# A spectral and mixture-of-experts kernel: width DFT and four centrings as four 64x64 tiles, first weight loads from the sixth sum on

## The reference

```python
x = x + _L0_conv_ref(_ln_c(x), L0_conv_w1_real, ...)   # 2D DFT, low modes times complex weights, inverse DFT
t = _to_tokens(x)
t = t + _L0_ffn_ref(_ln_t(t), L0_ffn_gate_w, ...)      # softmax over tokens, top 8 for each expert
x = _from_tokens(t, x)
x = x + _L1_conv_ref(_ln_c(x), L1_conv_w_d, ...)       # four sweeps, each row from the row before it
t = _to_tokens(x)
t = t + _L1_ffn_ref(_ln_t(t), L1_ffn_gate_w, ...)
```

## Time and profile before

| | |
|---|---|
| median of 3 runs | 577.56 us (576.42 to 582.18) |
| profiled execution, its own time | 579.15 us |
| its span, first to last instruction | 577.3 us |
| PE busy; PEld; DVE; ACT | 516.2; 462.0; 323.8; 275.8 us |
| first norm and width DFT in the trace | first centring 5.90 us, gate product 41.81 us |
| mean granted TensorE clock | 0.95 of full speed |

### The profile page before, as it was taken

How to read it: one execution, slowest core, us unless ns; L and a number is a source line. 1 busy time by engine, 2 the same in 40 slices (tenths; PEclk the granted TensorE clock), 3 DMA queues, 4 the chain that set the end, 5 groups by cost and what they waited for, 6 DMA issues and landing times.

```text
span 577.3 us, 25417 instructions
## 1 busy us (share of the span) xinstructions
PE 516.2 (89%) x11282; PEld 462.0 (80%) x11282; DVE 323.8 (56%) x767; ACT 275.8 (48%) x782; POOL 113.3 (20%) x240
## 2 busy tenths in 40 slices
PE   8878999768857999969999999889999999756997
PEld 8878998668747975859999888778899999756973
DVE  2757565833459537754544554445555445669626
ACT  3546554435577102654444444434446777748100
POOL 4000000000161000003333333643331033451000
PEclk9999999989996979988999999979999999976979
DMA  9940990051000000000000033410000244500007
GB/s 351 373 147 2 328 373 36 1 219 76 5 3 1 2 20 2 3 0 3 4 5 3 4 79 76 115 35 4 4 4 3 45 81 82 99 1 1 2 2 291
DMA packets 50259, 41.69 MB, mean 72 GB/s; under 512 B 44998, under 2 KB 45126, under 8 KB 48934
## 3 DMA queue, kind: packets, MB, share of 16 engines
q1 hardware_dynamic: 49304, 38.51, 20.8%
q0 software_dynamic: 704, 1.18, 0.9%
q10 hardware_dynamic: 144, 0.39, 0.2%
HBM read 27.49 MB, written 4.19 MB: 55 GB/s over the span
## 4 chain that ended last, share of the span: by engine, by line
PE 79%; DVE 8%; ACT 6%; POOL 4%; issue 3%; DMA 0%; SPq 0%; POOLq 0%; ACTq 0%; DVEq 0%
PE PS L766 40%; PE PS L550 6%; PE PS L494 5%; PE PS L735 5%; PE PS L591 3%; PE PS L532 3%; PE PS L685 3%; PE PS L473 2%; POOL RE L394 2%; PE PS L436 2%; POOL RCD L397 2%; PE PS L503 2%; DVE sums L1052 1%; PE PS L454 1%; PE PS L468 1%
## 5 line engine op out<-in xcount | busy, mean ns | idle before, releaser
L766 PE MATMUL PS<-RE,conv_sb 128*64 128x64 f32 x6048 | 231.2, 230 | 4.4 <-DVE RE L1151 4.0
L766 PEld LDWEIGHTS PS<-RE,conv_sb 128*64 128x64 f32 x6048 | 210.3, 139 | 25.4 <-DVE RE L1151 4.7
L901 ACT COPY PS<-convb_sb 128x64 f32<-128x64 f32 x504 | 108.2, 215 | 113.0 <-DVE RE L1163 102.6
L1163 DVE SCALAR_TENSOR_TENSOR RE<-PS,RCD 128x64 f32<-128x64 f32 x252 | 56.5, 224 | 58.3 <-PE PS L766 50.0
L406 POOL COPY RCD<-RE 128x128 f32<-128x128 f32 x126 | 37.1, 294 | 156.7 <-DVE RE L1163 156.6
L1163 DVE SCALAR_TENSOR_TENSOR RE<-PS,RE 128x64 f32<-128x64 f32 x126 | 32.6, 259 | 28.4 <-PE PS L766 21.0
L1163 DVE SCALAR_TENSOR_TENSOR RE<-PS,RB 128x64 f32<-128x64 f32 x126 | 28.3, 224 | 28.2 <-PE PS L766 28.2
L494 PE MATMUL PS<-warm 128*128 128x128 bf16 x418 | 35.6, 261 | 3.9 <-DVE warm L929 1.4
L494 PEld LDWEIGHTS PS<-warm 128*128 128x128 bf16 x418 | 32.6, 120 | 5.1 <-ACT RB L879 1.6
L394 POOL TENSOR_TENSOR RE<-RA 128x1024 f32<-128x1024 f32 x3 | 5.7, 1892 | 149.5 <-ACT RA L872 149.5
L550 PE MATMUL PS<-RE,RB 128*64 128x64 f32 x1024 | 32.2, 223 | 1.6 <-DVE RA L991 1.4
(11 more groups left out here) (117 smaller groups left out, 691.9 us busy)
## 6 DMA issues: line engine op xcount, KB each, us to landing
RE<-wspec SPq DMA_DIRECT2D x8, 2048.0 KB, 8.7
RA<-x_in SPq DMA_DIRECT2D x8, 512.0 KB, 7.4
RCD<-x_in SPq DMA_DIRECT2D x1, 4096.0 KB, 12.3
out<-RA SPq DMA_DIRECT2D x8, 512.0 KB, 2.7
RCD<-RB SPq DMA_DIRECT2D x58, 64.0 KB, 2.6
RE<-RCD SPq DMA_DIRECT2D x32, 80.0 KB, 2.6
conv_sb<-conv_w SPq DMA_DIRECT2D x1, 768.0 KB, 20.1
w_sb<-w SPq DMA_DIRECT2D x2, 264.0 KB
```

The lines of the kernel that those rows point to most:

```text
L766: m = pe.matmul(conv_bank(s, u, c)[o:o + OC], conv_sb[:, s, d, o:o + OC], prev, start=False, stop=(d == 2), skip_group_check=True)
L901: act.copy(banks_of, convb_sb[:, s:s + 1].unsqueeze(2).to_broadcast([P, c1 - c0, n])).then_inc(s_seed, 1)
L1163: dve.scalar_tensor_tensor(out=state[:, state_slot(s, u), b0:b1, 1:1 + HO], in0=conv_bank(s, u, c), scalar=0.0, in1=row_at(SRC[s], s, q, u ...
```

## The change

Three things change, all ahead of the gate product. The follower uses `quad` for all eight groups. The centring uses `quad` for groups 4 to 7 (`LN0_QUADS = 4`). Because `quad` splits the two halves over two banks, the normalisation of groups 4 to 7 and the drain read PSUM in another order; the drain becomes two copies of 512 columns. And chunks 0, 1 and 2 of the weights wait for sums 6, 7 and 8.

```diff
         def f1_pairs(g, i):
             o = RC.rearrange("p (t k r h) -> p t k r h", ...)[:, g // 4, :, :, 16 * (g % 4):16 * (g % 4) + 16]
-            return [(o, i.rearrange("p (h r k) -> p k r h", r=2, k=KY))]
+            return [(o[:, :, r].rearrange("p k (n a) -> p k n a", a=2),
+                     i.rearrange("p (a n r k) -> p r k n a", a=2, n=8, r=2)[:, r]) for r in range(2)]
...
-            for c in range(2):
-                sp.dma_start(RE[:, WCOLS * c:WCOLS * (c + 1)], wspec[c]).then_inc(s_wc[c], 16)
...
-            for c in range(2, NCH):
-                if c == 2:
-                    sp.wait_ge(s_sum, 8)
+            for c in range(NCH):
+                if c < 3:
+                    sp.wait_ge(s_sum, (6, 7, 8)[c])
...
-                        m = pe.matmul(blk(ln_slot(g), n), blk(RA, 8 * g + n), centre, start=True, stop=True)
+                        if g < LN0_QUADS:
+                            m = pe.matmul(blk(ln_slot(g), n), blk(RA, 8 * g + n), centre, start=True, stop=True)
+                        else:
+                            m = quad(2 * (g % 4), n, blk(RA, 8 * g + n), centre)
...
             def dft_w(g):
                 for n in range(8):
-                    m = pe.matmul(blk(ln_slot(g), n), blk(RD, 8 * g + n), fwd_w, start=True, stop=True)
+                    m = quad(2 * (g % 4), n, blk(RD, 8 * g + n), fwd_w)
...
+                            m = dve.tensor_tensor(
+                                tokens.rearrange("p (n a b c) -> p a n b c", a=2, b=2, c=C),
+                                ln_slot(g).rearrange("p (a n b c) -> p a n b c", a=2, b=2, c=C),
+                                r.rearrange("p (a n b) -> p a n b", a=2, b=2).unsqueeze(4).to_broadcast([P, 2, 8, 2, C]),
+                                ALU.mult)
```

## The result

The changed kernel takes 586.16 us, the median of 14 runs (582.05 to 590.8), against 576.39 us of the kernel before in the same 14 rounds: the ratio is 1.0159, with a 95% interval of 1.0123 to 1.0195. The ratios are taken over fast executions alone (without 590.8 us here), so they are not quite those of the medians. The changed kernel is slower, by 7 to 11 us. The forecast was 578.8 us and the range ended at 583, so both were wrong. The profiled execution took 587.83 us, and its span is 585.9 us against 577.3.

A forecast was written before the change was run, and what follows sets the result against it. PE and the normalisation ring bound the first stage by turns; after the change, late instruction blocks would. Quads -5.3 us and blocks +6.5 made 1.2 us more, against the median 577.56: 578.8 us, range 573 to 583.

The forecast's parts named there:

- The blocks: First stage: PE's 256-instruction blocks come late in followers 2 to 5 and 7, costing 6.5 us.
- What the loads do to a block: First stage: weight loads stretch a block from 3.9 us in quiet to about 5.5 us.
- The clock: First stage: PE idle waiting for a block drops to 1.2 GHz; 580.5 to 583.9 us, chance 0.15.
- the third rival: Clock falls in the wait for the last follower's block; 580.5 to 583.9 us, chance 0.15.
- the short fall: Half clock for 3.4 us over the last follower's end, gate product and row turns, losing 1.7 us.
- The half block: Four and a half added blocks move later block changes; inverse width DFT gaps change by 0.8 us either way.
- What the quads cost and save: First stage: 1.09 us from quad to quad against 1.79, at most 5.3 us gained.
- the gain with no late block: First stage: last follower ends at 35.4 instead of 40.71 us; 572.3 us, chance 0.15.
- The drain and the normalisation in halves: First stage: drain copies 1.16 us against 1.01, normalisation 1.23 against 1.22; extra 0.15 us paid once.
- The loads of weights: Moved chunks 0 to 2 land before their mixes need them, so waiting for them costs nothing.
- the price under load: While weights load, as in the mixing, a block takes about 5.5 us.

The follow-up runs named there:

- e3: The change, with weight chunks 0, 1 and 2 asked for only when all eight groups are drained; ratio 1.0034 to the kernel before.
- e9: The change, but with the last four centrings left whole, so followers alone are quads; ratio 0.9977 to the kernel before.
- e4: The kernel before plus 64 small dead matmuls (128 instructions) ahead of follower 6; ratio 1.0055.
- e11: The change plus 64 small dead matmuls between the last follower and the gate product, five whole blocks added; ratio 1.0153 to the kernel before.
- e6: The kernel before with followers and centrings 4 to 7 as two 64x128 tiles, plus 64 small dead matmuls ahead of the gate product; ratio 1.0289.
- e1: The change, with weight loads where they were before (chunks 0 and 1 right behind the image); ratio 1.0083 to the kernel before.
- e5: The kernel before with followers and centrings 4 to 7 as two 64x128 tiles, weight chunks early as before; ratio 1.0338.
- e12: The change, with followers alone as quads and the first chunks asked for only after the last drain; ratio 1.0034 to the kernel before.
- e2: The kernel before with only the weight loads moved to the sixth, seventh and eighth sums, tiles whole; ratio 0.9998.

## Why the prediction was wrong

- **The blocks.** Right in kind and in place: one for each lap, waits inside followers 2, 3, 4, 5 and 7, none in 6, 256 instructions apart. In quiet a block takes 3.55 to 3.83 us (e3), against 3.9 assumed; the first two came 1.2 and 1.3 us before their forecast times, with waits of 0.53 and 0.95 us where 1 us or more was forecast.
- **What the loads do to a block: mis-sized.** This is the first step that failed. Follower 4's block was priced at 4.15 us, since "the load is hardly under way", and those of 5 and 7 at 5.5 us, from the mixing. They took 6.02, 6.57 and 5.92: 18.5 us instead of 15.15. e3 shows that the loads are the cause. The first load was asked for at 25.15 us and the block at 25.21, and that block already took 6.02 us. The last block came at 43.72 us instead of 41.65.
- **The clock: the third rival came, earlier and longer, at its lower price.** The fall was priced for a wait of 3.3 us before the last follower, and given 0.15. It came three followers earlier, in the 3.51 us before follower 4's rest, which that mis-sized block had made so long; and it lasted 20.5 us, not 3.4 or 10. Its rows: quads of 1.9 us instead of 1.1, and row turns of 3.68 us, at 2.23 in e9. But up to the last block PE was held by its blocks and not by the slow quads, so that what the clock cost is some 1.7 us, the rival's price for the short fall. The chain to the first mix lost 5.2 us instead of 1.2: 2.1 us of the difference are the later last block, 1.7 the clock's. By that alone, 577.56 + 5.2 = 582.8 us, the time would have stayed in the range; what came behind the first mix took it out.
- **The half block: named, and not followed.** This is the second step that failed. The prediction saw that later block changes fall elsewhere and priced that at 0.8 us either way, by the inverse DFT alone. There it was 1.3 us more waiting than in the earlier trace rows. In the mixing, where weights are loading all the time, it cost some 3 us: 3.3 alone in e4 (ratio 1.0055), and 2.9 between the change and e11, where it is gone as in e6. This is the term that the sum lacked, and the largest behind the gate product. The same shows far behind, where it cost the change nothing (11.9 us late ahead of it and behind it): between 504 and 523 us the five kernels with a half block (the change, e1, e3, e4, e5) have issue waits of 1.19 to 2.4 us in the second layer's expert projections, and the other nine have none.
- **What the quads cost and save.** Right: 1.16 and 1.11 us each at the full clock. A last follower that ends at 35.4 us, the gain with no late block, was never seen. The nearest is e12, with followers alone as quads and no late block: its last one started at 35.53 us, at half the clock, and took 1.89.
- **The drain and the normalisation in halves.** Right, as the timelines of ACT and DVE show: two copies in 1.07 us (1.16 assumed), the normalisation in 1.22 us as in the earlier trace rows.

```profile
25.70 1.07 ACT L793 COPY RCD<-PS 128x512 f32<-128x512 f32 x2 [1.63 <-PE PS L454]
...
29.25 1.22 DVE L953 TENSOR_TENSOR RCD<-PS,rstd 128x1024 f32<-128x1024 f32 x1
```

- **The loads of weights.** Right that no mix waits for its chunk, and e2's whole time is that of before. Wrong that this settled the question: PE's blocks come later while weights move (e3), and with the new places of the loads the mixing waits some 1 us more (e2).

The rule of the Trainium skill's page "Runtime: NRT & Kernel Launch", section "Instruction fetch mechanics", that the fetch is mostly hidden, holds for the kernel before as a whole: it has three issue waits of over 0.15 us, in some 88 blocks (an estimate, 22564 / 256). It does not hold in the first stage of the change, where each of the five blocks from follower 2 on was waited for, 0.53 to 3.51 us.

What stays open: what decides whether the clock falls behind a wait, and why block changes half a block further on wait in the mixing, and those of before hardly do. In the change the late ones stand 6.1 to 6.4 us apart, the price under load, and those of before fall under the same loads. Which matmuls lie behind a change, and when the next chunk is asked for, both move with it; no run separates them.

## What to carry to other kernels

A tile that needs less of PE's time but four times the instructions is paid for by instruction blocks: count the instructions in each lap, compare 256 of them with the time that a block takes in that stage (here 3.6 to 3.8 us in quiet, 5.9 to 6.6 while large loads run), and expect a wait for the difference. Price what a wait can do to the clock along with the wait. And when an edit adds instructions ahead of a stage that runs close to this limit, add or take away whole blocks, or look at that stage again: half a block of dead work alone cost this kernel 0.55%.

## What the runs showed of the hardware

- The same 128 instructions of harmless work, hidden where they stand, made a stage that begins 16 us further on slower by 3.3 us (e4), and 128 more in e11 took 2.9 us off the mixing again. The waits' places are fixed to the instruction: in the change and e4 the same matmuls of the mixing wait, and in e11 the matmuls of the earlier trace rows again.
- The clock can stay at 1.2 GHz while the profile shows PE as busy: for 41.3 us in e5, with 39.15 us busy, in matmuls of 64x128 with 64 moving columns. The Trainium skill's page "TensorE: Matmul & The Clock Gate", section "What's actually happening", says that activity releases the throttle; this row does not agree: PE shows as busy, and the throttle stayed.
- Two 64x128 tiles did not run beside each other in these float32 products of 64 moving columns: 2.00 us for a group, against 2.05 us with 128x128 tiles and 1.16 us with four 64x64 ones. The Trainium skill's page "TensorEngine Tiling (Array Packing)", section "Theoretical Speedup", gives up to a factor of 2 for two tiles; e5 shows none. The shape alone does not decide it: the row turns (L436), transposes by tiles of that shape, took 2.23 us for 64 in the kernel before, 35 ns each.
